# Conditional convolution and quantised feed-forward network on one core: a shorter attention head, another split of the first aggregation, fillers between the first matmuls

## The reference, cut to what matters

```
h   = gelu(cond @ W0 + b0); h = gelu(h @ W1 + b1)
att = softmax(h @ W2 + b2)                      # (32 tiles, 8 experts)
agg_w = einsum('bk,koi->boi', att, weight)      # one 128x128 matrix a tile
agg_b = att @ bias_k
y   = agg_w @ x + agg_b                         # per tile, as bf16
q, s = round(y * inv / s), s = max|y * inv| / 127 by row      # for gate and for up
gate = (qg @ w_gate.T) * sg * s_wgate ; up = (qu @ w_up.T) * su * s_wup
inter = clip(silu(gate) * up, -10, 10)          # as bf16, quantised by row again
out  = x + (qi @ w_down.T) * si * s_wdown
```

## Time and profile before

| | us |
|---|---|
| median of three runs | 810.32 |
| profiled execution, its own time | 810.25 |
| its span, first to last instruction | 808.4 |
| TensorE busy | 795.6 (98%) |
| VectorE busy | 717.2 (89%) |
| ScalarE busy | 439.4 (54%) |

### The profile page before, as it was taken

One profiled execution on the slowest core, in us unless ns is written; L12 is line 12 of the kernel. 1 busy time (PEld: TensorE's weight loads), 2 busy tenths in 40 slices (PEclk: granted clock), 3 DMA queues, 4 the chain that ended last, 5 costly groups with the idle time before them and its releaser, 6 DMA issues.

```text
span 808.4 us, 9179 instructions
## 1 busy us (share of the span) xinstructions
PE 795.6 (98%) x3520; PEld 364.9 (45%) x3520; DVE 717.2 (89%) x811; ACT 439.4 (54%) x383; POOL 142.1 (18%) x136
## 2 busy tenths in 40 slices
PE   7999999999999999999999999999999999999997
PEld 4554444444444444444444444444444444444443
DVE  6996989999888988888988888988888988888967
ACT  5785344566645456645456645456655556655531
POOL 1602301112222201222211222210222210222000
PEclk9999999999999999999999999999999999999999
DMA  8996646455454444464544454444454544354332
GB/s 296 241 201 138 135 139 200 131 155 131 144 169 143 144 124 136 131 170 143 147 134 134 121 169 144 153 137 134 110 169 145 159 122 149 105 169 153 108 92 105
DMA packets 162820, 119.81 MB, mean 148 GB/s; under 512 B 151764, under 2 KB 151892, under 8 KB 153559
## 3 DMA queue, kind: packets, MB, share of 16 engines
q1 hardware_dynamic: 161048, 106.64, 44.4%
q0 software_dynamic: 1728, 12.58, 7.7%
HBM read 60.48 MB, written 33.55 MB: 116 GB/s over the span
## 4 chain that ended last, share of the span: by engine, by line
PE 87%; DVE 9%; ACT 2%; DMA 1%; issue 1%; DVEq 0%
PE up_ps L575 26%; PE gate_ps L575 25%; PE down_ps L659 22%; PE conv_ps L528 12%; DVE amax L1008 2%; DVE down_sc L1172 1%; DVE region L1119 1%; DMA xt<-x 1%; DVE region L1125 0%; DMA quT<-qu 0%; DVE xt L1181 0%; PE gate_ps L659 0%; DVE wd L1026 0%; PE conv_ps L533 0%; DVE qi L955 0%
## 5 line engine op out<-in xcount | busy, mean ns | idle before, releaser
L659 PE MATMUL down_ps<-wd,qiT 128*128 128x512 bf16 x896 | 211.2, 379 | 0.9 <-DVE down_sc L1172 0.9
L575 PE MATMUL gate_ps<-wg,qgT 128*128 128x512 bf16 x928 | 205.7, 379 | 0.5 <-ACT qgT L818 0.5
L575 PE MATMUL up_ps<-wu,quT 128*128 128x512 bf16 x896 | 202.4, 379 | 0.1
L1008 DVE TENSOR_REDUCE amax<-region 128x1 f32<-128x2048 f32 (+1 forms) x90 | 173.1, 1923 | 1.2
L426 POOL TENSOR_TENSOR prod<-wexp,att_bc 128x1024 f32<-128x1024 f32 x28 | 53.1, 1896 | 542.8 <-DVE region L1066 532.0
L659 PEld LDWEIGHTS down_ps<-wd,qiT 128*128 128x128 bf16 x896 | 87.4, 98 | 124.8 <-issue 28.5
L575 PEld LDWEIGHTS gate_ps<-wg,qgT 128*128 128x128 bf16 x928 | 90.6, 98 | 110.3 <-issue 1.1
L575 PEld LDWEIGHTS up_ps<-wu,quT 128*128 128x128 bf16 x896 | 87.6, 98 | 106.4 <-ACT quT L822 0.9
L765 ACT ACTIVATE qg<-region,recip 128x2048 f16<-128x2048 f32 x30 | 60.0, 2002 | 130.9 <-DVE recip L1018 130.9
L528 PE MATMUL conv_ps<-xt,aggw 128*128 128x512 f32 x244 | 117.0, 602 | 1.5 <-DVE aggw L995 0.9
L754 ACT ACTIVATE y<-conv_ps,aggb 128x512 bf16<-128x512 f32 x118 | 80.0, 685 | 61.1 <-PE conv_ps L528 56.7
(11 more groups left out here) (163 smaller groups left out, 569.4 us busy)
## 6 DMA issues: line engine op xcount, KB each, us to landing
xt<-x SPq DMA_DIRECT2D x30, 1024.0 KB, 4.8
out<-xt SPq DMA_DIRECT2D x29, 1024.0 KB, 4.0
wg<-w_gateT POOLq DMA_DIRECT2D x4, 1024.0 KB, 20.7
wu<-w_upT POOLq DMA_DIRECT2D x4, 1024.0 KB, 18.9
wd<-w_downT POOLq DMA_DIRECT2D x4, 1024.0 KB, 7.6
xt<-x SPq DMA_DIRECT2D x4, 512.0 KB, 4.4
invg_bc<-inv_gate SPq DMA_DIRECT2D x1, 1024.0 KB, 8.6
out<-xt SPq DMA_DIRECT2D x2, 512.0 KB, 2.9
```

The source lines that it names most:

```text
L575: last = nc.tensor.matmul(acc[:, n * BANK:(n + 1) * BANK], codes[:, k * P:(k + 1) * P], wts[:, k, n * BANK:(n + 1) * BANK], start=(k == 0) ...
L659: last = nc.tensor.matmul(down_bank(t, c), qiT_at(t)[:, k * P:(k + 1) * P], wd[:, k, c * BANK:(c + 1) * BANK], start=(k == ks[0]), stop=(k ...
L1008: nc.vector.tensor_reduce(amax[:, i:i + 1], src, axis=AX.X, op=ALU.max, apply_absolute_value=True).then_inc(max_ready, 1)
```

## The change

Five edits. The first group's softmax is cut short: `eatt0`, the exponentials, is written where the attention stands, and tile 0 to 3's aggregations and biases use these unnormalised numbers; the reciprocal of the sum is applied when y leaves PSUM, as the scale of the activation, and to the biases by one more multiplication. The sum and the reciprocal stand behind the aggregation's steps, ahead of its last addition. Second, b2 enters through TensorE, as a matmul of one row of ones with one row of b2, ahead of each logit matmul, so that VectorE's two bias additions go. Third, SPLIT is 5: VectorE adds up five experts of tile 0, TensorE three. Fourth, the four fillers of 512 columns before `aggregate_mm(0)` go; two of 512 columns stand before the first matmul, and narrow ones (128 columns) in the gaps: three behind hidden layer 1, three behind the first b2 row, two behind the logits, three behind `aggregate_mm(0)`. Fifth, the filler's memset comes before that of the ones.

```
-        SPLIT = 6
+        SPLIT = 5
...
+            def fill(n, width):
+                for _ in range(n):
+                    nc.tensor.matmul(down_ps[:, 0:width], filler[:, 0:P], filler[:, P:P + width], start=True, stop=True)
+            def logit_bias(g, n):
+                row = b2_s[0:1, :].unsqueeze(1).to_broadcast([1, n, K])
+                nc.tensor.matmul(by_tile(log_ps[g]), ones[0:1, :], row, start=True, stop=False)
+            def logit(g):
+                pe.wait_ge(att_dve, g + 1)
+                nc.tensor.matmul(log_ps[g], ones, group(hw, g), start=False, stop=True).then_inc(hid_mm, 1)
+            pe.wait_ge(filler_set, 1)
+            fill(2, BANK)
             pe.wait_ge(mlp_in, 16)
-            pe.wait_ge(ones_set, 1)
             nc.tensor.matmul(hid_ps, w0_s, embT_s, start=True, stop=True).then_inc(hid_mm, 1)
+            fill(3, P)
             pe.wait_ge(hid_act, 1)
             nc.tensor.matmul(hid_ps, w1_s, h1, start=True, stop=True).then_inc(hid_mm, 1)
...
+            pe.wait_ge(ones_set, 1)
+            pe.wait_ge(b2_in, 16)
+            logit_bias(0, FIRST)
+            fill(3, P)
+            logit(0)
+            logit_bias(1, B - FIRST)
+            logit(1)
+            fill(2, P)
...
-            pe.wait_ge(filler_set, 1)
-            for _ in range(4):
-                nc.tensor.matmul(bank(down_ps, 0), filler[:, 0:P], filler[:, P:P + BANK], start=True, stop=True)
             aggregate_mm(0)
+            fill(3, P)
             conv(0)
...
+                    norm = erec[:, t:t + 1] if t < FIRST else 1.0
                     nc.scalar.activation(y_at(t)[:, c * BANK:(c + 1) * BANK], conv_bank(t, c), ACT.Identity,
-                                         bias=aggb[:, t:t + 1]).then_inc(y_ready, 1)
+                                         scale=norm, bias=aggb[:, t:t + 1]).then_inc(y_ready, 1)
...
-                    act.wait_ge(att_dve, ATT[0])
+                    act.wait_ge(exp_done, 1)
...
-            nc.scalar.activation(group(eatt, 0), group(logits, 0), ACT.Exp).then_inc(exp_done, 1)
+            nc.scalar.activation(eatt0, group(logits, 0), ACT.Exp).then_inc(exp_done, 1)
...
+            nc.vector.memset(filler, 1.0).then_inc(filler_set, 1)
             nc.vector.memset(ones, 1.0).then_inc(ones_set, 1)
-            nc.vector.memset(filler, 1.0).then_inc(filler_set, 1)
...
-                nc.vector.tensor_tensor(z, raw, over_tiles(b2_s, n), ALU.add).then_inc(att_dve, 1)
+                nc.vector.tensor_reduce(top, raw, axis=AX.X, op=ALU.max).then_inc(att_dve, 1)
                 dve.wait_ge(att_dve, done + 1)
-                nc.vector.tensor_reduce(top, z, axis=AX.X, op=ALU.max).then_inc(att_dve, 1)
-                dve.wait_ge(att_dve, done + 2)
-                nc.vector.tensor_tensor(z, z, over_experts(top, n), ALU.subtract).then_inc(att_dve, 1)
+                nc.vector.tensor_tensor(z, raw, over_experts(top, n), ALU.subtract).then_inc(att_dve, 1)
+            def exp_sum(g, e, done):
+                total, inverse = tiles(esum, g), tiles(erec, g)
+                nc.vector.tensor_reduce(total, by_tile(e), axis=AX.X, op=ALU.add).then_inc(att_dve, 1)
                 dve.wait_ge(att_dve, done + 1)
                 nc.vector.reciprocal(inverse, total).then_inc(att_dve, 1)
...
             weighted(1, B - FIRST)
-            dve.wait_ge(b2_in, 16)
             softmax_in(0, FIRST, 2)
-            softmax_out(0, FIRST, 5)
+            dve.wait_ge(exp_done, 1)
...
                     op.then_inc(agg_step, 1)
+                exp_sum(0, eatt0, Z[0])
                 dve.wait_ge(agg_step, SPLIT)
                 dve.wait_ge(agg_mm, 1)
                 nc.vector.tensor_tensor(w, w, agg_ps[0], ALU.add).then_inc(agg_step, 1)
```

More of the change, by code:

```diff
@@ L150, in adaln_ffn @@
         eatt = qi32[:, B * K:2 * B * K]
+        eatt0 = att_bc[:, 0:FIRST * K]
         bprod = logits
@@ L271, in adaln_ffn @@
         INVU, SWG, SWU, INVI, SWD = 1, 2, 3, 4, 6
-        ATT, BIAS = (8, 15), (9, 16)
+        Z, ATT, BIAS = (4, 9), 12, (7, 13)
         PAGG = 3
@@ L424, in aggregate @@
                 if t <= POOLED + 1:
-                    pool.wait_ge(att_dve, ATT[0] if t < FIRST else ATT[1])
+                    pool.wait_ge(att_dve, ATT)
                 nc.gpsimd.tensor_tensor(prod[:, :, :], wexp[:, :, :], a, ALU.mult).then_inc(pagg_step, 1)
@@ L874, in _ @@
             quant_g(1)
-            act.wait_ge(att_dve, 12)
+            act.wait_ge(att_dve, Z[1])
             nc.scalar.activation(group(eatt, 1), group(logits, 1), ACT.Exp).then_inc(exp_done, 1)
@@ L961, in softmax_out @@
-            def softmax_out(g, n, done):
-                e, total, inverse = by_tile(group(eatt, g)), tiles(esum, g), tiles(erec, g)
-                dve.wait_ge(exp_done, g + 1)
-                nc.vector.tensor_reduce(total, e, axis=AX.X, op=ALU.add).then_inc(att_dve, 1)
+                nc.vector.tensor_tensor(z, raw, over_experts(top, n), ALU.subtract).then_inc(att_dve, 1)
+            def exp_sum(g, e, done):
+                total, inverse = tiles(esum, g), tiles(erec, g)
+                nc.vector.tensor_reduce(total, by_tile(e), axis=AX.X, op=ALU.add).then_inc(att_dve, 1)
@@ L965, in softmax_out, with biases_first @@
                 dve.wait_ge(att_dve, done + 1)
                 nc.vector.reciprocal(inverse, total).then_inc(att_dve, 1)
-                dve.wait_ge(att_dve, done + 2)
-                nc.vector.tensor_tensor(by_tile(group(att_bc[:, :], g)), e, over_experts(inverse, n), ALU.mult).then_inc(att_dve, 1)
-                dve.wait_ge(att_dve, done + 3)
-            def biases(g, n):
+            def biases_first():
+                prods = by_tile(group(bprod, 0))
+                dve.wait_ge(bk_moved, 1)
+                nc.vector.tensor_tensor(prods, by_tile(eatt0), over_tiles(bk_kept, FIRST), ALU.mult).then_inc(bias_prod, 1)
+                dve.wait_ge(bias_prod, 1)
+                nc.vector.tensor_reduce(tiles(aggb[:, :], 0), prods, axis=AX.X, op=ALU.add).then_inc(bias_prod, 1)
+                dve.wait_ge(bias_prod, 2)
+                dve.wait_ge(att_dve, BIAS[0] - 1)
+                nc.vector.tensor_tensor(tiles(aggb[:, :], 0), tiles(aggb[:, :], 0), tiles(erec, 0), ALU.mult).then_inc(att_dve, 1)
@@ L972, in biases, with attention_rest @@
+            def attention_rest():
+                g, n = 1, B - FIRST
+                dve.wait_ge(exp_done, 2)
+                exp_sum(1, group(eatt, 1), ATT - 3)
+                dve.wait_ge(att_dve, ATT - 1)
+                nc.vector.tensor_tensor(by_tile(group(att_bc[:, :], g)), by_tile(group(eatt, g)),
+                                        over_experts(tiles(erec, g), n), ALU.mult).then_inc(att_dve, 1)
+                dve.wait_ge(att_dve, ATT)
                 prods = by_tile(group(bprod, g))
-                dve.wait_ge(bk_moved, 1)
@@ L1184, in _ @@
             aggregate_first()
-            biases(0, FIRST)
+            biases_first()
             diagonals(2)
@@ L1204, in _ @@
             diagonals(3)
-            softmax_in(1, B - FIRST, 9)
+            softmax_in(1, B - FIRST, 7)
             quant_g(1)
             quant_u(0)
-            softmax_out(1, B - FIRST, 12)
-            biases(1, B - FIRST)
+            attention_rest()
             quant_g(2)
```

4 lines of the change are left out of this document (2 added, 2 removed).

## The result

The changed kernel is slower: 810.53 us median (809.69 to 811.91, 18 runs) against 808.59 (807.68 to 810.58, 18 runs) for the kernel before beside it, ratio 1.0021, 95% interval 1.0013 to 1.0029. (All ratios here are taken over all executions; they are not the quotient of the two medians, from which they can differ because the times stand in groups.) I had forecast 808.2. The time lies inside the range; the sign is wrong. The times of before were also not what three runs had shown: 11 of 18 lie at 807.7 to 809.2 and 7 at 810.1 to 810.6, and the profiled execution (810.25) was of the upper group. The changed kernel has no execution under 809.6. Its profiled execution took 810.31, so the two profiled spans (808.4 and 808.5) are equal: the loss can't be read from this pair alone.

What follows compares the result with a forecast made beforehand. TensorE was taken as the bound, never without work from gate(1) at 35.59 us, so a gain must bring that moment forward. 810.25 - 2.25 (tile 1's product earlier) + 0.15 (given back) = 808.15, say 808.2 us; range 806.6 to 810.6.

Steps and rivals of the forecast that it cites:

- Step 1: First group's softmax on VectorE: start on tile 0's weights at 6.75, ready for the last addition at 9.06 instead of 9.89.
- Step 2: TensorE's branch into tile 0's last addition (bias rows, three diagonals) grows; conv(0) between 9.5 and 10.7, taken as 9.7.
- Step 3: Fillers leave TensorE hardly standing from 3.0 to about 7.8 us, so its clock rises to 2.4 GHz ahead of conv(0).
- Step 4: From conv(0) to tile 0's fourth maximum at the higher clock: end at 16.96 against 18.89, 1.9 earlier.
- Step 5: Second group's softmax on VectorE: tile 1's product, held by GpSimd's broadcast until 22.75, ends at 25.04, 2.25 us earlier.
- first rival: Tile 1's product gets ahead of GpSimd's broadcast and ends near 22.4; 3.4 us less, 806.9; chance 0.17.
- Step 6: From tile 1's product to gate(1): all 2.25 us earlier, 0.15 given back further on; sum 808.15, say 808.2.
- The second: Clock still rises in the middle of conv(0); only the shorter second softmax gains, 0.4 to 0.8; centre 809.8; chance 0.25.
- The third: Slower: diagonal branch with the clock rising only behind conv(0), which starts 0.3 late; 813, or 811.3 with half; chance 0.10.

Runs made afterwards that it cites:

- b_again: The kernel before, unedited, measured and profiled a second time: median 809.71 us, ratio 1.0002; its profiled execution took 807.34.
- b_pad: Kernel before plus 21 fillers of 16 columns (14 ahead of the first matmul, 7 behind tile 0's aggregation), filler's memset first: 809.17 against 808.33, ratio 1.0016.
- b_warm: Kernel before plus fillers of 512 columns in the earlier TensorE gaps, filler's memset first: 808.09 against 808.33, ratio 0.9995.
- padded kernels: Kernel before plus 21 or 18 fillers of 16 columns: 809.17 against 808.33, ratio 1.0016; 810.27 against 808.60, ratio 1.0012.
- held kernels: Edited kernels, from before or changed, with GpSimd's broadcasts held back until VectorE has finished tile 1's product: ratios 0.9995, 0.9985, 0.9979, 0.9978.

## Why the prediction was wrong, step by step

Two steps of the chain failed, 2 and 3, and the level from which I reckoned was not that of the kernel.

- **Step 1, right.** Start on tile 0's weights 6.76 (forecast 6.75), VectorE ready at 8.91 (9.06).
- **Step 2, failed: the branch through the row of ones and the diagonals was priced too low.** I wrote conv(0) between 9.5 and 10.7 and took 9.7; it is 11.08. I had named the right branch, since the addition waits 1.74 us for TensorE's part, but its terms were too small even for the lower clock (addition at 9.9 to 10.1, measured 10.65), and I then chose the higher clock. The second logit matmul starts at 6.98 instead of 5.74: it comes 1.04 behind the row of ones, which itself starts only at 5.94, behind the first logits. So the copy is at 8.13, not 7.82. From the last diagonal's end (9.35) to the addition are 1.30 us and not 0.43 + 0.25, since TensorE works on the three diagonals from 8.92 to 10.54. I bounded a chain (row of ones, logits, copy, diagonals, matmuls) by its links' nearest rows and did not line it up with the other branch at the clock that the trace showed there. Undoing the order or the row brings conv(0) to 10.34 and 9.98: shown. In the time the row is worth 0.7 us (809.29 against 810.03 beside it) and the order 0.06 to 0.16%, the latter with overlapping intervals.
- **Step 3, failed: the rise ahead of conv(0) did not come.** In the changed kernel's two profiles and in the five variants that keep narrow fillers behind the logits, conv(0)'s loads come to 190 ns at 12.8 to 15.4 us. Without any filler it is 15.4 and 16.1. With three or four wide ones directly ahead of tile 0's aggregation they are there by 11.0 in 7 of 11 profiles and at 12.1 to 14.8 in the other four. I took time without a gap for enough; here TensorE hardly stood from 3.0 to 8.3 us, with short fp32 matmuls and fillers of 128 columns, and the clock was still the lower one at conv(0). That wide fillers make the rise likelier is shown by times too: the kernel before without them has no execution under 809.1, and the changed kernel without the second row of ones has ratio 1.0004 with narrow fillers and 0.9993 with wide ones, on two chips, with overlapping intervals. What decides in a single execution stays open.
- **Step 4.** Its arithmetic was right, for the kernel before: from conv(0)'s start to the end of the fourth maximum are 7.29 us in b_again (10.40 to 17.69), forecast 7.26. One thing I had at nothing costs: y with the reciprocal as scale operand takes 0.78 us instead of 0.69 per bank, 16 times, of which four stand in ScalarE's way ahead of tile 1's product.
- **Step 5.** The broadcast as a lock was right, and it also acts in the kernel before. A product of tile 1 ahead of it takes 2.29, behind it 2.9 to 3.6, and the operations before the product can be held too. The rule of the Trainium skill (SBUF — State Buffer, "Who interferes with whom") that issue order decides who blocks holds in both orders: VectorE's add of 2.35 us in the earlier trace rows, GpSimd's broadcast of 4.22 in b_again. Of the sixteen profiles of kernels that are not held, the product came first in b_again alone. Its place is worth less than the 1.15 us between my first rival and the forecast. In b_pad the clock rises early and the product is behind the broadcast, and gate(1) is at 32.91, only 0.2 later than in b_again; in b_warm, where the broadcast also holds VectorE's subtraction (2.33 us instead of 0.39), it is at 33.84:

```profile
20.31 2.30 POOL L437 PARTITION_BROADCAST invu_bc<-wu  x1 [9.30 <-issue]
21.05 3.57 DVE L1031 TENSOR_TENSOR wd<-wd,invg_bc 128x2048 f32<-128x2048 bf16 x1 [0.67 <-ACT wd L759]
32.91 3.63 PE L578 MATMUL up_ps<-wg,wd 128*128 128x512 bf16 x15 [0.70 <-ACT wd L759]
```
```profile
20.04 2.33 DVE L967 TENSOR_TENSOR qi<-qi,qiT 128x224 f32<-128x224 f32 x1
33.84 3.63 PE L583 MATMUL up_ps<-wg,wd 128*128 128x512 bf16 x15 [0.70 <-ACT wd L762]
```

- **Step 6.** gate(1) is 0.51 earlier instead of 2.25. And there is a cost that I had not thought of: the row of ones, the third expert and nine more fillers lengthen TensorE's stream, and its fetch moves from 125 to 120 us, where a wait of 1.2 and 0.5 follows.
- **The level of before.** I took 810.25 as the kernel and 808.35 as the exception, "a bound on what the clock alone can bring". It was the other way round: the median of 18 is 808.59. Right for the reason, I said that this run showed an early rise; I did not ask how often it happens, and that the change might take it away. So the sign of the result hangs on this level: set against the profile of 810.25, the changed kernel's 810.31 is no loss.
- **The rivals.** The second, with the rise in the middle of conv(0), was nearest to the changed kernel's own profile (rise at 12.84, 810.31 where it had 809.3 to 810.3), though its conv(0) at 10.4 to 10.7 was too early as well. The third had the mechanism that the median shows (the four wide fillers gone) with the wrong price: not 811.3 to 813 by a later rise, but the loss of the executions in which gate(1) comes 2.9 us earlier. The Trainium skill (TensorE: Matmul & The Clock Gate, "What's actually happening") says that the point of the rise varies by 500 ns either way from run to run; the traces agree that it varies, but by more: at or before conv(0)'s first loads at 10.37 in one execution of the kernel before, and after 13.87 in another.

## What to carry to other kernels

Where the times of one kernel stand in groups, find out which of them the profile is of before pricing a change, and ask whether the change keeps the way into the better one. When a sum waits for two branches, shortening one is worth nothing beyond the slack, and every instruction added to an engine that feeds the other must be placed in its queue at the clock that rows show there. A copy for later work must not stand ahead of what the first result waits for.

## What the runs showed of the hardware

- One and the same kernel at one and the same point, conv(0): weight loads at 337 or 190 ns, by execution (before, b_again). The granted-clock column reads 1.00 in both.
- With a 16 KB fetch of instructions beside it, a store of 512 KB took 4.8 us to landing instead of 2.6 (changed kernel, before). With fetches at 116 and 117 single executions of the padded kernels took 812.4 to 813.1; none of these was profiled, and the unpadded kernel before has a single 812.2 too, on another chip. Why is open.
- A broadcast of 2048 columns on GpSimd took 2.30 us in all four held kernels and 2.30 to 3.34 in the others in which it came first, whether VectorE waited for it or not; it took 4.22 where it waited for VectorE's product (b_again).
